# A convolution block on channels-last images: four neighbouring pixels per partition, and a tridiagonal matrix for the convolution across columns

## The reference, cut to what matters

```python
v = _gn(x)                                # 32 groups of channels, mean and variance over rows, columns and a group's 24 channels
xc = conv2d(v as NCHW, conv1_w, conv1_b)  # 1 x 1, 768 -> 16 channels
pooled = mean(xc over rows and columns)   # -> gates g: softmax over the best 2 of 4 experts
for i in range(4):                        # expert i, f = 2 ** i
    up = resize(xc, rows * f, columns * f, bilinear)
    experts.append(resize(conv2d(up, convl_w, convl_b), back to 64 x 64, bilinear))   # 3 x 3, 16 -> 16 channels
out = sum(experts[i] * gate[i])
out = x + conv2d(out, conv2_w, conv2_b)   # 1 x 1, 16 -> 768 channels
```

## Time and profile before

| | |
|---|---|
| time, median of 3 runs | 1454.27 us (1450.56 to 1458.54) |
| the profiled execution | span 1451.0 us from first to last instruction; its own time is not given beside it |
| TensorE, matmuls | 1189.7 us busy, 82% of the span |
| VectorE | 1029.3 us, 71% |
| ScalarE / GpSimd | 661.9 us, 46% / 313.9 us, 22% |
| DMA | 188162 packets, 540.01 MB, mean 372 GB/s |
| mean granted TensorE clock | 0.879 of full speed |

### The profile page before, as it was taken

How to read it: one execution, slowest core, us unless ns; L and a number is a source line. 1 busy time by engine, 2 the same in 40 slices (tenths; PEclk the granted TensorE clock), 3 DMA queues, 4 the chain that set the end, 5 groups by cost and what they waited for, 6 DMA issues and landing times.

```text
span 1451.0 us, 24055 instructions
## 1 busy us (share of the span) xinstructions
PE 1189.7 (82%) x8700; PEld 814.9 (56%) x8700; DVE 1029.3 (71%) x2747; ACT 661.9 (46%) x1549; POOL 313.9 (22%) x381
## 2 busy tenths in 40 slices
PE   0679999988987999789968899887787899779863
PEld 0466676656654777466546666555555665445531
DVE  6869988678469897764797884569766755636654
ACT  3578999553423797545225784411551352100110
POOL 1083003403041000340540001065004104344100
PEclk9989999999986999799978999978898898667865
DMA  9798897499999999999999998999999999999999
GB/s 344 256 359 318 301 370 288 176 392 319 399 366 416 409 389 349 378 395 387 392 412 411 390 377 288 388 396 402 416 390 344 399 411 414 417 416 410 401 416 388
DMA packets 188162, 540.01 MB, mean 372 GB/s; under 512 B 12810, under 2 KB 12810, under 8 KB 188044
## 3 DMA queue, kind: packets, MB, share of 16 engines
q1 hardware_dynamic: 118140, 336.75, 61.4%
q10 hardware_dynamic: 69904, 201.74, 34.9%
HBM read 337.12 MB, written 201.33 MB: 371 GB/s over the span
## 4 chain that ended last, share of the span: by engine, by line
PE 45%; DMA 23%; DVE 16%; ACT 5%; issue 5%; SPq 4%; POOL 1%; ACTq 0%; DVEq 0%; POOLq 0%
PE ring_ps L680 16%; DMA x_sb<-in_x 12%; DMA out<-x_sb 10%; PE conv_ps L750 10%; DVE x_sb L1010 9%; PE img_ps L697 8%; PE ring_ps L781 8%; DVE stats L926 7%; SPq L521 3%; ACT xT L803 2%; PE ring_ps L710 1%; SPq L494 1%; PE ring_ps L769 1%; ACT unread_squares L831 1%; ACT unread_copy L833 1%
## 5 line engine op out<-in xcount | busy, mean ns | idle before, releaser
L1010 DVE TENSOR_TENSOR x_sb<-x_sb,ring_ps 128x768 f32<-128x768 f32 x512 | 462.1, 950 | 299.5 <-PE ring_ps L781 215.8
L926 DVE BATCH_NORM_STATS2 stats<-x_sb 128x6 f32<-128x192 f32 x1792 | 473.0, 344 | 36.7 <-DMA x_sb<-in_x 26.8
L803 ACT COPY xT<-ring_ps 128x1024 f32<-128x1024 f32 x384 | 377.0, 1012 | 194.1 <-PE ring_ps L680 130.7
L781 PE MATMUL ring_ps<-w,es 128*128 128x512 f32 (+1 forms) x1024 | 335.8, 447 | 126.0 <-DVE x_sb L1010 107.7
L680 PE MATMUL ring_ps<-ident,x_sb 128*128 128x128 f32 x3072 | 402.4, 284 | 25.2 <-DVE x_sb L1010 10.4
L680 PEld LDWEIGHTS ring_ps<-ident,x_sb 128*128 128x128 f32 x3072 | 351.5, 146 | 101.9 <-issue 56.0
L781 PEld LDWEIGHTS ring_ps<-w,es 128*128 128x128 f32 x1024 | 190.9, 232 | 250.1 <-DVE x_sb L1010 169.2
L643 POOL TENSOR_TENSOR band<-taps,masks 128x640 f32<-128x640 f32 (+1 forms) x112 | 132.9, 1203 | 515.7 <-PE conv_ps L750 511.9
L697 PE MATMUL img_ps<-xT,w 128*32 128x256 f32 x3072 | 216.2, 389 | 16.2 <-ACT xT L803 15.2
L750 PE MATMUL conv_ps<-xc,band 128*128 128x1 f32 (+8 forms) x1120 | 221.4, 346 | 0.7 <-POOL band L643 0.7
L750 PEld LDWEIGHTS conv_ps<-xc,band 128*128 128x128 f32 x1120 | 159.0, 198 | 69.9 <-issue 67.3
(11 more groups left out here) (94 smaller groups left out, 361.1 us busy)
## 6 DMA issues: line engine op xcount, KB each, us to landing
x_sb<-in_x SPq DMA_DIRECT2D x128, 1536.0 KB, 11.3
out<-x_sb ACTq DMA_DIRECT2D x256, 768.0 KB, 9.8
x_sb<-in_x SPq DMA_DIRECT2D x172, 768.0 KB, 9.3
w_rep<-in_L_conv_conv_w ACTq DMA_DIRECT2D x1, 384.0 KB
wl_raw<-in_L_conv_convl_w SPq DMA_DIRECT2D x8, 9.0 KB
gate_w<-in_L_conv_H_w SPq DMA_DIRECT2D x8, 0.2 KB
w_raw<-in_L_conv_conv_w SPq DMA_DIRECT2D x1, 48.0 KB
b_raw<-in_L_conv_conv_b SPq DMA_DIRECT2D x2, 3.0 KB
```

The costliest lines, as they stand in the source:

```text
L781: last = nc.tensor.matmul(flat_ps[:, buf, part], es4[:, q, (i % 4) * P:(i % 4 + 1) * P], w2[:, part], start=True, stop=True)
L803: nc.scalar.copy(xT[:, at % XT], ring_ps[:, TURN["T", a, n] % RING]).then_inc(xT_copied, 1)
L926: ins = nc.vector.bn_stats(stats[:, c, g, :], group)
L1010: nc.vector.tensor_tensor(x_sb[:, n, 2 * half + q % 2, :], x_sb[:, n, 2 * half + q % 2, :], flat_ps[:, TURN["E", b, t] % RING, 0:D], ALU.a ...
```

## The change

- Which pixels share a partition: `x_v` and `out_v` now take 4 neighbouring columns of one row (`q` is the fastest part of the column index), so the run of a partition in a whole-slot load is 4 pixels, 12 KB, and in a half slot 2 pixels, 6 KB. Consecutive partitions of a DMA start 24 KB apart. Bytes, number and order of the DMAs stay.
- The 8 partition blocks of `img_ps` are now the column modulo 8, and the free axis is 64 rows by 8 groups of columns. The column taps therefore run across partitions and the row taps along the free axis.
- The convolution: one full matrix `near` (own columns and both neighbours, for 5 kinds of row tap), and `sides` with narrow 32-column pieces for the wrap between column groups (7 of 8 groups) and for the image's first and last column. `conv` has 3 parts instead of 7: NEAR 4 matmuls, WRAP 10 narrow ones, EDGE 10 narrow ones and one full one (8 columns). 25 matmuls per image instead of 35. The two sides write output partitions 0 to 31 and 96 to 127.
- GpSimd: `near` and `sides` are single buffers, zeroed once; per image 16 small `place` instructions on 32 partitions each instead of 7 builds on 128 and 2 memsets. `weigh_taps` has its own buffer and no longer waits for the convolution before; the first `place` waits until all three parts of the image before have been used.
- `PE_ORDER`: C items 0 to 6 become 0 to 2, placed among the same other items: C.0 stays where it was, C.1 and C.2 stand where later ones of the seven stood. The other orders, `TRANSFERS` too, are the same.

```diff
@@ -28,7 +28,6 @@
-BANDS = 3
...
@@ PE_ORDER @@
-T3.19 M3.17 T3.20 M3.18 T3.21 M3.19 T3.22 M3.20 T3.23 M3.21 T2.0 M3.22-23 T2.1 Z2 C3.0-2 T2.2-4 C3.3-6 T2.5 M2.0-1
...
+T3.19 M3.17 T3.20 M3.18 T3.21 M3.19 T3.22 M3.20 T3.23 M3.21 T2.0 M3.22-23 T2.1 Z2 C3.0 T2.2-4 C3.1-2 T2.5 M2.0-1 X3.0
...
-UP, HERE, DOWN, FROM_ABOVE, FROM_BELOW, TOP, BOTTOM = range(7)
-MAT_ROW_TAP = [LEFT, MID, RIGHT, LEFT, RIGHT, LEFT_EDGE, RIGHT_EDGE]
-SAME, ABOVE, BELOW = range(3)
-MAT_MASK = [SAME, SAME, SAME, ABOVE, BELOW, SAME, SAME]
-MAT_ORDER = [HERE, FROM_ABOVE, UP, FROM_BELOW, DOWN, TOP, BOTTOM]
-NM = len(MAT_ORDER)
+BLOCKS = WW // NH
+NEAR, WRAP, EDGE = range(3)
+NM = 3
+ROW_KINDS = (MID, LEFT, RIGHT, LEFT_EDGE, RIGHT_EDGE)
...
-def blk_ranges(m):
-
-    return {UP: (slice(1, NB), slice(0, NB - 1)), HERE: (slice(0, NB), slice(0, NB)),
-            DOWN: (slice(0, NB - 1), slice(1, NB)), FROM_ABOVE: (slice(0, 1), slice(NB - 1, NB)),
-            FROM_BELOW: (slice(NB - 1, NB), slice(0, 1)), TOP: (slice(0, 1), slice(0, 1)),
-            BOTTOM: (slice(NB - 1, NB), slice(NB - 1, NB))}[m]
+def row_ranges(ax):
+
+    return {LEFT: (slice(1, HH), slice(0, HH - 1)), MID: (slice(0, HH), slice(0, HH)),
+            RIGHT: (slice(0, HH - 1), slice(1, HH)), LEFT_EDGE: (slice(0, 1), slice(0, 1)),
+            RIGHT_EDGE: (slice(HH - 1, HH), slice(HH - 1, HH))}[ax]
+
+
+def side_ranges(part, side):
+
+    if part == EDGE:
+        end = slice(BLOCKS - 1, BLOCKS) if side else slice(0, 1)
+        return end, end
+    before, after = slice(0, BLOCKS - 1), slice(1, BLOCKS)
+    return (before, after) if side else (after, before)
...
-    slots_of = "b (q p j bb) w c -> b p j (bb w) q c"
-    x_v = x.rearrange(slots_of, q=QN, p=2, j=4, bb=2)
-    out_v = out.rearrange(slots_of, q=QN, p=2, j=4, bb=2)
+    slots_of = "b (j r) (d p q) c -> b p j (r d) q c"
+    x_v = x.rearrange(slots_of, j=4, d=BLOCKS, p=2, q=QN)
+    out_v = out.rearrange(slots_of, j=4, d=BLOCKS, p=2, q=QN)
...
-        masks = sb("masks", [P, 3, NH, R])
+        mask = sb("mask", [P, NH, R])
...
-        band = sb("band", [P, BANDS, NT, NH, R])
+        near = sb("near", [P, NT, NH, R])
+        sides = sb("sides", [P, 2, 2, NT, 2, R])
+        weighed = sb("weighed", [P, NT * NT * R])
...
-        conv_v = conv_ps[:, :].rearrange("p (k w) -> p k w", w=WW)
-        xc_v = xc[:, :, :].rearrange("p b (k w) -> p b k w", w=WW)
+        conv_v = conv_ps[:, :].rearrange("p (r d) -> p r d", d=BLOCKS)
+        xc_v = xc[:, :, :].rearrange("p b (r d) -> p b r d", d=BLOCKS)
...
-            link(nc.gpsimd.memset(masks[:, :, :, :], 1.0))
-            for kind, shift in ((SAME, 0), (ABOVE, -1), (BELOW, 1)):
-                keep_where(masks[:, kind], -R * shift, [[-R, NH], [0, R]], 1)
-                keep_where(masks[:, kind], R * shift + R - 1, [[R, NH], [0, R]], -1)
+            link(nc.gpsimd.memset(mask[:, :, :], 1.0))
+            keep_where(mask[:, :, :], 0, [[-R, NH], [0, R]], 1)
+            keep_where(mask[:, :, :], R - 1, [[R, NH], [0, R]], -1)
...
-            def weigh_taps(b, bi):
+            nc.gpsimd.memset(near[:, :, :, :], 0.0)
+            nc.gpsimd.memset(sides[:, :, :, :, :, :], 0.0).then_inc(bands_zeroed, 1)
+            pool.wait_ge(bands_zeroed, 1)
...
+            def place(into, rows, column_tap, own):
+
+                count = own.stop - own.start
+                full = [2 * R, NT, count, R]
+                return nc.gpsimd.tensor_tensor(into, taps[rows, :, column_tap].unsqueeze(2).broadcast_to(full),
+                                               mask[rows, own].unsqueeze(1).broadcast_to(full), ALU.mult)
+
+            quarter = [slice(2 * R * q, 2 * R * q + 2 * R) for q in range(QN)]
             for bi, b in enumerate(B_ORDER):
                 pool.wait_ge(gates_ready, b // 4 + 1)
                 if bi:
                     pool.wait_ge(band_ready, NM * bi)
-                    pool.wait_ge(band_used, NM * bi - BANDS + 1)
-                weigh_taps(b, bi)
-                for part, m in enumerate(MAT_ORDER):
-                    n = NM * bi + part
-                    if n >= BANDS and part:
-                        pool.wait_ge(band_used, n - BANDS + 1)
-                    blocks = slice(0, 1) if m == TOP else slice(NH - 1, NH) if m == BOTTOM else slice(0, NH)
-                    if m in (TOP, BOTTOM):
-                        link(nc.gpsimd.memset(band[:, n % BANDS], 0.0))
-                    full = [P, NT, blocks.stop - blocks.start, R]
-                    nc.gpsimd.tensor_tensor(band[:, n % BANDS, :, blocks],
-                                            taps[:, MAT_ROW_TAP[m]].unsqueeze(2).broadcast_to(full),
-                                            masks[:, MAT_MASK[m], blocks].unsqueeze(1).broadcast_to(full),
-                                            ALU.mult).then_inc(band_ready, 1)
+                weigh_taps(b)
+                if bi:
+                    pool.wait_ge(band_used, NM * bi)
+                for q in range(QN):
+                    own = slice(2 * q, 2 * q + 2)
+                    if q:
+                        place(near[quarter[q], :, 2 * q - 2:2 * q], quarter[q], RIGHT, own)
+                    if q < QN - 1:
+                        place(near[quarter[q], :, 2 * q + 2:2 * q + 4], quarter[q], LEFT, own)
+                    place(near[quarter[q], :, own], quarter[q], MID, own)
+                place(near[quarter[0], :, NH - 2:NH - 1], quarter[0], RIGHT, slice(1, 2))
+                place(near[quarter[-1], :, 1:2], quarter[-1], LEFT, slice(NH - 2, NH - 1)).then_inc(band_ready, 1)
+                first, last = slice(0, 1), slice(NH - 1, NH)
+                place(sides[quarter[-1], 0, 0, :, 0:1], quarter[-1], LEFT, last)
+                place(sides[quarter[0], 0, 1, :, 1:2], quarter[0], RIGHT, first).then_inc(band_ready, 1)
+                place(sides[quarter[0], 1, 0, :, 0:1], quarter[0], LEFT_EDGE, first)
+                place(sides[quarter[-1], 1, 1, :, 1:2], quarter[-1], RIGHT_EDGE, last).then_inc(band_ready, 1)
...
             def conv(b, part):
-                m = MAT_ORDER[part]
                 n = BI[b] * NM + part
-                if part == 0:
+                if part == NEAR:
                     pe.wait_ge(xc_copied, AI[b] + 1)
                     if BI[b]:
                         pe.wait_ge(lo_ready, BI[b])
                 pe.wait_ge(band_ready, n + 1)
-                for ax in (MID, LEFT, RIGHT, LEFT_EDGE, RIGHT_EDGE):
-                    blk_out, blk_in = blk_ranges(m)
-                    col_out, col_in = column_ranges(ax)
-                    last = nc.tensor.matmul(
-                        conv_v[:, blk_out, col_out], band[:, n % BANDS, ax].rearrange("p h r -> p (h r)"),
-                        xc_v[:, XC_PLACE[b], blk_in, col_in],
-                        start=(part == 0 and ax == MID), stop=(part == NM - 1 and ax == RIGHT_EDGE))
+                def own_blocks(ax):
+                    row_out, row_in = row_ranges(ax)
+                    return nc.tensor.matmul(conv_v[:, row_out], near[:, ax].rearrange("p h r -> p (h r)"),
+                                            xc_v[:, XC_PLACE[b], row_in], start=(ax == MID), stop=(ax == RIGHT_EDGE))
+
+                def end_blocks(ax, side):
+                    row_out, row_in = row_ranges(ax)
+                    at_out, at_in = side_ranges(part, side)
+                    block = slice(P - 2 * R, P) if side else slice(0, 2 * R)
+                    return nc.tensor.matmul(
+                        conv_v[block, row_out, at_out], sides[:, part - 1, side, ax].rearrange("p h r -> p (h r)"),
+                        xc_v[:, XC_PLACE[b], row_in, at_in], start=False, stop=False)
+
+                for ax in ROW_KINDS:
+                    if part == NEAR:
+                        if ax != RIGHT_EDGE:
+                            last = own_blocks(ax)
+                        continue
+                    for side in range(2):
+                        last = end_blocks(ax, side)
+                if part == EDGE:
+                    last = own_blocks(RIGHT_EDGE)
                 last.then_inc(band_used, 1)
```

More of the change, by code:

```diff
@@ L132 @@
+E13.16-28 C12.0 E13.29-31 X15.0 X15.1 E15.0-4 E15.5-6 C12.1 E15.7-10 E15.11-13 X15.2 E15.14-15 X15.3 E15.16-19 C12.2
+E15.20-31 X12.0-1 E12.0-13 X12.2 E12.14-15 X12.3 E12.16-31
 """
@@ L439, in program @@
         gates_ready = sem("gates_ready")
+        bands_zeroed = sem("bands_zeroed")
         band_ready = sem("band_ready")
@@ L560, in _ @@
             nc.gpsimd.memset(b2_raw[:, :], 0.0).then_inc(bias_zero, 1)
-            link(nc.gpsimd.memset(masks[:, :, :, :], 1.0))
-            for kind, shift in ((SAME, 0), (ABOVE, -1), (BELOW, 1)):
-                keep_where(masks[:, kind], -R * shift, [[-R, NH], [0, R]], 1)
-                keep_where(masks[:, kind], R * shift + R - 1, [[R, NH], [0, R]], -1)
+            link(nc.gpsimd.memset(mask[:, :, :], 1.0))
+            keep_where(mask[:, :, :], 0, [[-R, NH], [0, R]], 1)
```

(15 more changed lines are left out.)

82 lines of the change are left out of this document (35 added, 47 removed).

## The result

After the change the median is 1431.8 us (three runs, 1429.9 to 1437.0; a fourth, disturbed run of 1608 us at a lower granted clock is left out), before 1452.4 us beside it on the same chip. The ratio is 0.9857, with a 95% interval of 0.9823 to 0.9892: 21 us faster, 1.4%, where 59 us and 4% were forecast (1454 to 1395).

The account below looks back on a forecast made before the run. TensorE was taken to bound 145 to 290 us, the DMA nearly everything after. Span 1451.0 - 12 (convolution) - 30 (DMA) - 18 (lost time) - 3 (start) + 4 (wait) = 1392 us, so 1395 us; range 1362 to 1435.

Parts of the forecast that it names:

- a matrix set: One image's convolution on TensorE at full clock: 7.0 us in place of 13.2, if the narrow side matmuls run side by side.
- the wait at image 14: TensorE waits 4 us (bounds 0 and 14) for GpSimd's `near` at image 14, where fresh gates are needed; added to the span.
- the start: SyncE's issue of the first loads: fewer descriptors fill its ring less, 3 us won out of at most 22.5.
- the roof: DMA rate when both queues always have work: 416 GB/s before, near 427 GB/s in the last stage after.
- Rival 3: Convolution's sides run one by one on TensorE and the DMA gains little: 1433 us, chance 0.08.
- rival 1: DMA engines cut the long runs up again, so only TensorE's part is left: 1428 us, chance 0.15.
- Rival 4: Queues alternate by packet, so 12 KB loads slow 6 KB stores: up to 1468 us, chance 0.06, mild form another 0.06.
- rival 2: TensorE's part is worth more, half of `conv`'s share of the chain, 73 us: about 1365 us, chance 0.15.
- I take a quarter of the lost time, 18 us: From 290 us on, the other 14 images' lighter convolution gives back a quarter of 73 us of lost DMA time.
- Images 3 and 2 in the TensorE-bound stage, 12 us: From 145 to 290 us TensorE binds; two images convolved there save 6.2 us each (bounds 5 and 12 in all).
- I take 30 us: Transfers from 290 us on: longer runs cost less per packet, 2.6% or 28 us of 1088, up to 46, floor 0.
- the sign to watch: DMA share after the 145 us stage should stay 0.97 or more; below, the places' round trip is the bound.

Follow-up runs that it names:

- e3: Kernel after with 6 KB runs in loads and stores alike (two pairs of neighbouring pixels per partition; mixes the wrong pixels): 1438.1 us, ratio 0.9892 to the kernel before.
- e5: Only the slot loads, reloads and stores, without computation or weight loads, with the kernel after's pixel view (12 KB and 6 KB runs): 1281.3 us, ratio 0.8817.
- e2: Kernel after with the old pixel view (3 KB runs), so the new convolution alone; mixes the wrong pixels: 1450.2 us, ratio 0.9977 to the kernel before.
- e1: Kernel before with only the new pixel view of loads and stores (12 KB and 6 KB runs); mixes the wrong pixels: 1440.4 us, ratio 0.9906.
- e4: Only the slot loads, reloads and stores, without computation or weight loads, with the kernel before's pixel view (3 KB runs): 1319.4 us, ratio 0.9069.
- e11: e8 with each late `es_lo` in VectorE's order moved forward to where `es_hi` is ready: 1420.0 us, ratio 0.9777 to the kernel before.
- e8: Kernel after with the small weight loads issued among slot loads 5 to 13 instead of behind the 13th: 1425.5 us, ratio 0.9813 to the kernel before.
- e7: Kernel after with VectorE's statistics over 6 of each group's 24 channels: 1420.2 us, ratio 0.9768 to the kernel before.
- e6: Kernel after with only 3 of the 25 convolution matmuls per image: 1431.2 us, ratio 0.9851 to the kernel before.

## Why the prediction was wrong

The direction was right and every part measured by itself came out close: a matrix set 6.6 us (7.0), the wait at image 14 4.17 us (4), the start 3.05 us (3), a `place` 517 ns (525), a 12 KB packet 461 ns (457 to 460), the roof 425 GB/s (427), the transfers alone 2.9% (2.6%). The result lies inside the stated range of 1362 to 1435 us, but at its end, where it was stretched to take in rivals 1 and 3, and that is luck. Rival 3 (sides in a row, little from the DMA) gives 1433 us, nearest to the result, and rival 1 (runs cut again) 1428, both by mechanisms that did not take place: the convolution takes 6.6 us and not 10.9, and 12 KB runs go as one packet. Rival 4 (unequal turns) is refuted by e3 and e5, rival 2 (the convolution worth more) by e2. A slip without weight: 172 reloads of 768 KB are 135 MB, not 132.

The sum is redone as the prediction made it, from bytes and the roof. Before, 87.5 MB went out in the first 290 us and 452.5 MB behind them: 1088 us at the roof and 73 lost. After, (324 + 300) GB/s x 145.1 us = 90.5 MB in the first 290 us; the other 449.5 MB at 425 GB/s take 1058 us of the 1138 spent, and 80 are lost. That is -7 (3.0 MB sooner at 416 GB/s), -23 (449.5 MB at 425 and not 416) and +7: 23 us of span, where 59 were forecast.

- **"I take a quarter of the lost time, 18 us"**: the step that failed. The lost time, in which the 4 us of the wait lie too, was to fall by 14 us and rose by 7, which is 21 of the 36 us that the sum was off. I read the 73 us as idle time that a faster TensorE would give back. But a reload waits for a store and an add for that reload, so an item that is ready sooner waits for the same transfer. In e2 the adds' waits for reloads grew by 40 us while the kernel gained 3; with half the bytes the same convolution gained 36. Counted like the sum, e2 moves (319 + 295) GB/s x 145.1 us = 89.1 MB in the first 290 us and the other 450.9 MB, 1084 us at 416 GB/s, in 1159.9 us: 76 us are lost against 73, so behind 290 us the lighter convolution gave nothing back.
- **"Images 3 and 2 in the TensorE-bound stage, 12 us", and the start, 3**: 7 us in place of 15. Image 3's 6.2 us are there at its `es_hi` (10.0 of lead = 3.8 + 6.2). Image 2's are not (8.9 us of lead at its `es_hi`), and it was put in the wrong stage: before the change it is convolved from 320 to 337 us, behind the window that ends at 290, and from 290 to 326 us the DMA share is already 1.02. A gain inside a stage counts only if the next stage can use the head start: in e2 7.1 us at image 3 are 1.3 at image 8. The 3 us of the start are not the packets' alone: in e1 the next slot load goes out 1.5 us sooner.
- **"I take 30 us" for the DMA**: 23 us, and by the prediction's line 28 for a roof of 427 GB/s, which was 425. Nor is it free of the rest: in e1's profiled run (319 + 285) x 145.1 = 87.6 MB and then 452.4 MB at 424 GB/s leave 87 us lost in place of 73. That run is the slowest of e1's eight; at their median some 82 are lost. So of 21 us that the packets saved 9 to 14 became idle queues. In the kernel after 80 are lost, so the convolution brought its 7 us beside the long runs (2.9 MB sooner) in the first 290 us and hardly any behind them.
- The Trainium skill, "DMA: Bandwidth & Descriptors", section "Why small descriptors are slow", would have given about 20 us by its overhead per packet, an estimate. The 23 us of the kernel lie nearer to that than to my 30, and the 38 us between e4 and e5 farther away.
- The wait of 4 us, the 3 us of the start and nothing for GpSimd elsewhere held.

The prediction named the sign to watch: a DMA share below 0.97 means that the bound has moved to the round trip of the places, and that the 18 us were put wrong. It was 0.96 from 290 to 580 us and 0.98 to 1.00 behind that, so the sign came in one stage of four. The mechanism stood there as a doubt, and had no rival with a price: with the 18 us at nothing the forecast would have been 1413 us.

**The version that beats both** is e11, at 1420.0 us, 2.2% below the kernel before with the same result. Of its 12 us beyond the change some 6 come from the start (e8) and 5 from the earlier `es_lo`; neither step is clear of noise by itself, the two together are.

What stays open: how the 80 us of lost time after 290 us divide between the number of places, the order of the transfers and VectorE's work (e7 shows that the last holds some of it). More places or another `TRANSFERS` were not tried.

## What to carry to other kernels

When a transfer queue is full and the engines are 70 to 80% busy, as here, an engine's saving is not worth its busy time: 96 us less of convolution brought 3 us alone and 7 beside the longer runs. Count it only in stretches where that engine binds and the next stage can use the head start, and check by the timeline that the work lies in that stretch. Before giving an engine "a share of the lost time", look at which wait would grow in its place; here it was the adds' wait for reloads, a single line in the list of waits. To test it, halve the bytes of both kernels and see whether the difference appears.

## What the runs showed of the hardware beside this

- **The granted clock fell as TensorE's idle time grew.** Its mean was 0.879, 0.850 and 0.818 (before, after, e6), and a part of the saved work came back: `conv` fell by 221.4 - 67.7 - 57.4 = 96.3 us of busy time, and all other groups of TensorE together rose by 17, of which the E matmuls are 10.4 (335.8 to 346.2).
- **The issue of a load waits for packets before it.** In the kernel before, the first three slot loads took 0.4 to 0.6 us each to issue, and six of the next ten 3.75 to 4.02 us, in which 509 to 527 packets land, about the 512 of one slot load. With a quarter of the packets the first nine were issued by 5.7 us. But then the small loads met the same wait: eight of 9 KB took 35.0 us in place of 16.2. Spread among the slot loads (e8) they let the 14th go out 10.9 us sooner, where the longer runs alone (e1) gave 1.5.
- **Two full queues shared the engines by bytes here, not by packets.** 680 packets of 6 KB ran beside 348 of 12 KB in 20 us of the kernel after, 4.18 and 4.28 MB.
